# The attention stage l1_attn of an eight-phase model: scores ahead of weighing, sign counts in spans of 14 one pair of heads sooner, the Gram product one group later, the maxima spread anew

## The reference

```python
q, k, v = (proj(Wq, bq), proj(Wk, bk), proj(Wv, bv))
scores = jnp.einsum('bhqd,bhkd->bhqk', q, k) / jnp.float32(np.sqrt(dh))
attn = jax.nn.softmax(scores, axis=-1)
sr = MIN_SPARSITY + (1.0 - MIN_SPARSITY) * jax.nn.sigmoid(entropy_ema - entropy_threshold)
k_keep = jnp.maximum(1, (L * (1.0 - sr)).astype(jnp.int32))
order = jnp.argsort(-attn, axis=-1)
rank = jnp.argsort(order, axis=-1)
keep = rank < k_keep[None, :, None, None]
w = jnp.where(keep, attn, jnp.float32(0.0))
w = w / (jnp.sum(w, axis=-1, keepdims=True) + 1e-10)
out = jnp.einsum('bhqk,bhkd->bhqd', w, v)
...
return out @ Wo.T + bo
```

## Time and profile before

| | us |
|---|---|
| median of 3 runs (2890.3 to 2893.26) | 2890.33 |
| the profiled execution | 2892.41 |
| its span, first to last instruction | 2890.6 |
| stage l1_attn, about | 600 to 1390 of the span |
| over_ready of sequences 3 and 4 | 996.39 and 1083.19 |
| one full pass, from these two | 86.8 |

### The profile page before, as it was taken

One profiled execution on the slowest core, in us unless ns is written; L12 is line 12 of the kernel. 1 busy time (PEld: TensorE's weight loads), 2 busy tenths in 40 slices (PEclk: granted clock), 3 DMA queues, 4 the chain that ended last, 5 costly groups with the idle time before them and its releaser, 6 DMA issues.

```text
span 2890.6 us, 42636 instructions
## 1 busy us (share of the span) xinstructions
PE 2257.9 (78%) x13648; PEld 1725.6 (60%) x13648; DVE 1915.9 (66%) x5803; ACT 1083.5 (37%) x3168; POOL 666.0 (23%) x900
## 2 busy tenths in 40 slices
PE   3999999963576677657699999499579999999604
PEld 2777777741455565556566666377347777778501
DVE  5567453245888888886566666454567777777597
ACT  1333333328767677762122222134223333333100
POOL 3333121032755556656000000431000000000000
PEclk9999999965555555555699999599689999999658
DMA  3111000020000000000100000210100000000000
GB/s 106 37 30 39 21 20 25 1 80 19 9 10 8 12 12 7 6 1 1 41 1 0 0 0 0 46 39 21 56 10 1 0 0 0 0 0 0 1 0 15
DMA packets 57561, 49.02 MB, mean 17 GB/s; under 512 B 6840, under 2 KB 55704, under 8 KB 56856
## 3 DMA queue, kind: packets, MB, share of 16 engines
q1 hardware_dynamic: 54340, 45.50, 4.9%
q10 hardware_dynamic: 3040, 1.38, 0.3%
HBM read 19.78 MB, written 1.05 MB: 7 GB/s over the span
## 4 chain that ended last, share of the span: by engine, by line
PE 52%; DVE 29%; issue 7%; ACT 6%; POOL 3%; SPq 1%; ACTq 1%; DVEq 0%; DMA 0%; POOLq 0%
PE bank L1142 8%; PE bank L1558 4%; PE bank L1550 4%; PE bank L1551 4%; DVE weights L2546 4%; PE bank L1024 3%; PE bank L1004 3%; ACT rope_c L3349 2%; ACT rope_s L3349 2%; PE bank L1296 2%; PE bank L1280 2%; PE bank L1123 2%; DVE small L2584 2%; PE bank L1017 2%; PE bank L1099 2%
## 5 line engine op out<-in xcount | busy, mean ns | idle before, releaser
L1464 PE MATMUL bank<-V,probsT 128*128 128x9 f32 x1024 | 236.1, 364 | 76.5 <-ACT probsT L3360 76.5
L1464 PEld LDWEIGHTS bank<-V,probsT 128*128 128x128 f32 x1024 | 226.2, 328 | 113.9 <-ACT probsT L3360 94.3
L2187 DVE TENSOR_REDUCE nmax<-bank 128x4 f32<-128x1024 f32 x144 | 176.1, 1223 | 111.9 <-PE bank L1099 110.8
L3177 ACT ACTIVATE probs<-bank,nmax 128x256 f32<-128x256 f32 x256 | 119.0, 470 | 221.9 <-DVE nmax L1939 221.9
L1558 PEld LDWEIGHTS bank<-weights,hid 128*128 128x128 f32 x1152 | 151.6, 193 | 80.0 <-issue 76.7
L3415 ACT ACTIVATE hid<-bank 128x512 f32<-128x512 f32 x144 | 85.7, 597 | 284.3 <-PE bank L1551 272.3
L2780 DVE TENSOR_TENSOR hid<-hid,bank 128x512 f32<-128x512 f32 x144 | 98.6, 687 | 128.4 <-PE bank L1558 124.2
L1558 PE MATMUL bank<-weights,hid 128*128 128x128 f32 x1152 | 152.9, 277 | 13.4 <-DVE hid L2780 11.1
L1004 PE MATMUL bank<-big,qT 128*128 128x256 f32 x512 | 141.9, 404 | 15.3 <-DVE x L1860 14.8
L1550 PE MATMUL bank<-O,weights 128*128 128x512 f32 x288 | 149.6, 601 | 2.6 <-DVE big L2720 2.6
L1551 PE MATMUL bank<-O,weights 128*128 128x512 f32 x288 | 148.8, 599 | 0.0
(11 more groups left out here) (615 smaller groups left out, 5658.2 us busy)
## 6 DMA issues: line engine op xcount, KB each, us to landing
qT<-parts SPq DMA_DIRECT2D x276, 32.0 KB
big<-V SPq DMA_DIRECT2D x192, 32.0 KB
big<-parts SPq DMA_DIRECT2D x180, 32.0 KB
weights<-in_weights_l_ffn SPq DMA_DIRECT2D x1, 4832.0 KB, 14.0
weights<-in_weights_l_attn SPq DMA_DIRECT2D x1, 3904.0 KB, 12.8
weights<-in_weights_l_ffn SPq DMA_DIRECT2D x1, 3628.0 KB, 14.3
qT<-V SPq DMA_DIRECT2D x96, 32.0 KB
weights<-in_weights_l_ffn SPq DMA_DIRECT2D x1, 2304.0 KB, 7.8
```

What stands on the lines that cost most here:

```text
L1464: last = mm(pb[1][:, t * S + h * wide:t * S + (h + 1) * wide], probsT[:, h % 2, at:at + P], values_of(b, k)[:, h * wide:(h + 1) * wide], s ...
L2187: V_.tensor_reduce(to, scored.rearrange("p (i a n) -> p i a n", i=HPG, n=n), AX.X, ALU.max, negate=True).then_inc(score_max.sem, 1)
L3177: last = nc.scalar.activation(probs[:, h % 3, at:at + n], bank[:, at:at + n], ACT.Exp, bias=nmax[:, h, t:t + 1], accum_out=rowsum[:, h, t: ...
```

## The change

The order of instructions is rewritten on PE, DVE and ACT, and in each of the three counts two rows go from DVE to ACT; no new kind of instruction is made.

```diff
-ROWS_DVE = 6
+ROWS_DVE = 4
...
# PE, l1_attn
                         for j in range(h, h + 2):
+                            if now(n + 2) and j + 3 < H:
+                                l1_scores(n + 2, j + 3)
                             if now(n):
                                 l1_weigh(n, j)
-                            if now(n + 2) and j + 3 < H:
-                                l1_scores(n + 2, j + 3)
                         if now(n + 3):
                             if h == 2:
                                 l1_turn_keys(n + 3)
-                            if h == 4:
+                            if h == 6:
                                 l1_gram(n + 3)
...
# DVE, l1_attn
-                    l1_pair(n, 2, (), (3,))
-                    l1_pair(n, 4, (4,), (5, 6, 7))
+                    l1_pair(n, 2, (3,), ())
+                    l1_pair(n, 4, (4,), (5,))
                     if now(n + 1):
                         try_between(n + 1, 2)
                         count_above(n + 1, 2)
+                    if now(n + 2):
+                        l1_max(n + 2, 6)
+                        l1_max(n + 2, 7)
+                    l1_pair(n, 6, (8,), ())
                     if now(n + 3):
                         l1_gram(n + 3)
-                    l1_pair(n, 6, (8,), (9, 10, 11))
+                    if now(n + 2):
+                        l1_max(n + 2, 9)
+                        l1_max(n + 2, 10)
+                    if now(n + 1):
+                        settle_on(n + 1)
                     if now(n + 3):
                         l1_spread(n + 3)
-                    if now(n + 1):
-                        settle_on(n + 1)
                     if now(n + 2):
+                        l1_max(n + 2, 11)
                         l1_max(n + 2, 12)
-                        l1_max(n + 2, 13)
                     for i in range(4):
                         if now(n + 1):
                             count_kept(n + 1, 8 * i, 8 * i + 8)
-                        if now(n + 2) and i < 2:
-                            l1_max(n + 2, 14 + i)
+                        if now(n + 2) and i < 3:
+                            l1_max(n + 2, 13 + i)
...
# ACT, l1_attn
                         if now(n + 1) and h < 4:
-                            first = ROWS_DVE + h // 2 * 13
-                            l1_count(n + 1, 1, first, first + 13)
-                        if now(n + 1) and 6 <= h < 10:
-                            first = ROWS_DVE + (h - 6) // 2 * 13
-                            l1_count(n + 1, 2, first, first + 13)
+                            first = ROWS_DVE + h // 2 * 14
+                            l1_count(n + 1, 1, first, first + 14)
+                        if now(n + 1) and 4 <= h < 8:
+                            first = ROWS_DVE + (h - 4) // 2 * 14
+                            l1_count(n + 1, 2, first, first + 14)
```

## The result

The changed kernel takes 2930.89 us (median of 4 runs, 2929.51 to 2933.21), the kernel before 2891.8 beside it (2890.3 to 2893.39): a ratio of 1.0136, 95% interval 1.0118 to 1.0153. It is 1.4% slower. The forecast was 2932.

The account below looks back on a forecast made before the run. No engine is full; a pass is one loop of waits, turning on M to T, T to O and M's place. Five full passes at +6.3, plus 3.7, 3.5 and 3, give +41.7: median 2932, 1.4% slower, range 2916 to 2946.

Parts of the forecast that it names:

- M: End of the second interpolation, behind DVE's second narrowing; forecast 0.8 us earlier (0.3 to 1.2), as POOL holds DVE's operations.
- O: The over_ready from which passes are followed, after DVE reads the doubts; at 1083.19 in the kernel before.
- M to T: Second interpolation's end to third narrowing, ACT's signs and two heads between: forecast 0.8 us shorter, 16.8 against 17.6.
- T: DVE's third narrowing, after ACT's third count; at 1058.28 in the kernel before, forecast about 16.8 us after M.
- T to O: Third narrowing to over_ready: 7.9 us longer, 32.85 against 24.91, with PE's heads 8 to 15 and the products behind T.
- The strict reading: Second narrowing: no DVE progress until GpSimd stops; M 0.7 us later than before, each full pass 1.5 us more, 2939.5.
- rival 3: DVE, not PE, ends T to O because scores and weighings overlap ACT better: 2924 us, slower by 1.2%; 12%.
- The low bound: With PE's chain free, DVE reaches the doubts' read at T+26.8 and T to O grows by 6.3 us; 2924 in all.
- then -1.7 a pass: Correction to a full pass in us if, on PE between T and O, the exponentials do not hold the scores.
- First and second count, the Gram product: nothing: First count and narrowing, second count (ends about 1030.7 still) and the later Gram product: 0 us gained or lost.
- rival 1: Both narrowings: small DVE operations not held by POOL; full pass -1.8 us, 2881 in all, faster; 5%.
- rival 2: Only the second narrowing is not held by POOL; full pass +0.4 us, other passes some +6, 2898 in all; 6%.

Follow-up runs that it names:

- Experiment 4: Changed kernel with POOL waiting for the second interpolation before its last two groups of candidates: 2892.55 us, ratio 1.0009 to the kernel before.
- experiment 6: Kernel before with only POOL's wait for the second interpolation added: 2891.13 us, ratio 0.9998.
- Experiment 2: Kernel before with only the third count's signs moved early, behind heads 4 and 5 and heads 6 and 7, still 13 a half: 2933.09 us, ratio 1.0149.
- experiment 3: Changed kernel with weighing put back ahead of the scores on PE: 2916.65 us, ratio 1.0087 to the kernel before.
- experiment 1: Changed kernel with the third count's signs back behind heads 6 and 7 and heads 8 and 9: 2921.41 us, ratio 1.0111 to the kernel before.
- experiment 7: Changed kernel with the third count's signs back behind heads 6 and 7 and those heads' maxima ahead of the second narrowing: 2902.49 us, ratio 1.0039.
- Experiment 8: Kernel before with only the scores put ahead of each weighing on PE: 2892.97 us, ratio 1.0003.
- experiment 5: Changed kernel with both POOL's wait for the second interpolation and weighing ahead of the scores: 2878.37 us, ratio 0.9958 to the kernel before.

## Why the prediction was right

Steps in its order, pass 3 of the changed kernel unless another is named:

| step | forecast | measured |
|---|---|---|
| M behind O | 43.5 (0.8 sooner) | 43.8 (0.5 sooner) |
| M to T | 16.8 | 16.75 |
| T to O | 32.85 | 32.9 |
| DVE's wait for the products | 5.2 | 5.11 |
| DVE's wait for the doubts' sum | 1.6 | 1.42 |
| ACT idle ahead of the third count | about 6 | 6.34 |
| a full pass | +6.3 | +6.5 (mean of five: 6.3, 6.8, 6.4, 6.7, 6.2) |
| pass 5, pass 6, pass -1 | +3.7, +3.5, +3 | +2.8, +3.05, +3.0 |
| the stage | +41.7 | about +41 |
| the median against before | +41.7 | +39.1 |

**M.** The count of POOL's ends was right: from the start of the narrowing it had seven left, seven operations were held, one for each, and the last four ran free behind POOL's last end. The variant with one operation at each end (M at 1040.35 of before's time, O+43.96) was the closer one; I had taken the middle between it and two operations slipping in. Experiments 4 and 6 show the cause by taking POOL away: 2.3 us instead of 9.4, and 2.3 instead of 6.1. The Trainium skill (GPSIMD Engine Reference, section 8, Key points) says that GpSimd contends with VectorE instructions of two SBUF inputs or in a 2-port mode, and these runs agree. The strict reading, no progress until GpSimd stops, was mine, and it is not borne out: seven operations passed during POOL's stretch, each at the end of one instruction. One reading of the rows was loose: the 0.18 us that the prediction quotes for a quiet POOL is the operation at 1036.57, which slipped in while POOL ran; beside a quiet POOL the row at 1040.49 shows 0.19, so nothing hangs on it.

**T to O.** The chain of PE's starts came out within 0.1 us up to the weighing of head 14. The read of the doubts was 0.2 sooner than the sum (T+28.3 instead of 28.47) and what follows it 0.2 longer (4.6 instead of 4.38). Experiments 2 and 3 show the two parts of the price: the signs' place puts heads 8 and 9 and the products behind them, and the scores' place adds 2.5 on top. Experiment 2, which has neither the scores' new place nor the settling ahead of the products' take, is as slow as the change, so these two seem to cancel there; no run parts them. That DVE ends this stretch in the changed kernel (rival 3) is out, because DVE stands idle for 1.42 ahead of the read and PE's sum ends that wait. The low bound built on it was not a bound, however: it kept DVE's wait for the products at 5.2, and in experiment 3, where DVE does end the stretch, that wait is shorter too and the read comes at T+26.0 instead of T+26.8. The prediction's "then -1.7 a pass", for scores that wait for no exponentials, was too small as well: in pass 3 it is -2.4.

**First and second count, the Gram product: nothing.** No run here isolates the spans of 14 or the Gram product, but the trace agrees. The first narrowing ends at O+17.5 in both kernels, and the second starts at O+34.4, where the forecast had O+34.5. DVE waits 4.76 for the Gram product (forecast 4.5), and then still 0.81 for ACT's counts ahead of T; so the product is off the path, but by no more than 0.8 us. The spread of the maxima is not nothing by itself, as experiments 1 and 7 show, only in this arrangement.

**The end passes** 5 and 6 were 0.9 and 0.45 below the forecast, the five full ones in sum 0.8 above it. Here the sums were better than their parts. In pass 5, M came 1.9 sooner, M to T was 1.3 shorter and T to O 5.9 longer, where the forecast had 0.8, 0.8 and 5.3; in pass 6 the three are 0.7 sooner, 1.0 longer and 2.8 longer, where it had T to O alone, by 3.5. That they nearly cancel is luck.

**The rest of the kernel.** In the two profiled executions the changed kernel enters the stage 3.8 us later and gets 7.9 us back behind it, in code that is the same in both. In the windows 100 to 200 and 300 to 400 the granted clock is 0.98 and 0.97 instead of 1.00; where the 7.9 us come from was not looked into. Both are of the size by which single executions differ (23 of the kernel before lie between 2885.65 and 2895.84) and were no part of the sum.

**Rivals 1 and 2** needed the small operations free. Experiment 4 is what rival 2 described, reached by moving POOL: it gives 2892.55, where rival 2 said 2898. Its full passes cancel as the rival had it (0.0 to +1.3, but for one at -1.3, against +0.4). Its end passes did not cost the rival's 6 us: passes 5 and 6 are 0.8 and 2.0 shorter than before.

## What to carry over

Before a step is given to one engine sooner, find what delivers its input: here a handful of tiny operations was slowed by another engine's long ones, so the new place paid its price (eight heads behind T) and got almost nothing back, until one wait on the disturbing engine turned 1.4% of loss into none and, with the older order on PE, into a gain of 0.4%. The same wait in the old order was worth nothing, so a wait is judged by who is late next. How much of the 0.4% belongs to the signs' place and how much to the maxima behind the narrowing, which let DVE start it 3.8 us sooner, is not shown: no run has POOL's wait with the signs' place alone. The places of a maximum, a sign and a score in three lists are one decision: undoing one alone, as in experiment 1, measures the pair that it breaks.

## What was not expected of the hardware

TensorE's clock stood at its lower level, 1.2 GHz (granted 0.50), through all passes of the kernel before. In the profiled execution of every other kernel it rose to the upper one, 2.4 GHz, for some 4 us in one or more of the full passes, once or twice in each. The changed kernel has this in its pass 4, right behind T, where the weighing of head 8 took 1.09 us instead of 1.87:

```profile
1178.70 1.09 PE L1464 MATMUL bank<-V,probsT 128*128 128x9 f32 x8
```

Experiment 8 has it in the middle of a pass. Windows of that kernel, columns as in the earlier trace rows:

```profile
948.00:956.80 8.80, 7.52 (x32) 6.27 (x32) 7.30 (x13) 3.72 (x16) 7.28 (x7) 0.51 0.12 35
956.80:961.00 4.20, 4.11 (x28) 3.25 (x28) 4.17 (x20) 4.20 (x18) 4.00 (x1) 0.88 0.10 25
961.00:975.00 14.00, 8.30 (x35) 6.83 (x34) 8.10 (x31) 13.29 (x53) 7.28 (x8) 0.50 0.00 1
```

PE had been busy 7.52 of the 8.80 us ahead of it. The pass was no shorter (87.0), because PE waits for ACT there (4.97 idle at 966.02). Where the rise falls behind T and PE's chain is on the path, it does shorten the pass. Experiment 4 has two neighbouring full passes with and without it:

```profile
911.71:997.57 85.86, 59.94 (x258) 49.29 (x258) 72.25 (x278) 66.33 (x255) 52.61 (x53) 0.54 0.03 10
997.57:1084.51 86.94, 60.82 (x258) 49.96 (x258) 72.25 (x279) 66.47 (x256) 52.60 (x53) 0.50 0.03 10
```

The first is 1.1 us shorter, nearly all of it between T and O (31.8 against 32.8). In experiment 5 a pass with the rise at T takes 83.6 us, its neighbours without it 84.5 and 84.35. So a stretch is best compared between passes at the same clock. What makes the clock rise there was not tried.
